# The low part of the next head's FFN weights: two VectorE subtractions in place of four on GpSimd

## The reference

```python
xn = layernorm(x)
q, k, v = (xn @ Wq.T), (xn @ Wk.T), (xn @ Wv.T)          # 16 heads of 32
attn = softmax(causal(q @ k.T / sqrt(32)))
s = (attn @ v) @ Wo.T
hidden = fwht(silu(xn @ W1.T) * (xn @ W3.T))             # [b, t, 2048]
g = silu(hidden @ W2.T)
out = x + s * g
```

## Time and profile before

| what | value |
|---|---|
| median of three runs | 1041.69 us |
| profiled execution, its own time / its span | 1041.96 us / 1040.2 us |
| busy, share of the span: PE / DVE / ACT / POOL | 95% / 69% / 54% / 32% |
| weight loads of PE (PEld) | 76% |
| the two stretches of heads | about 96 to 400 us and 620 to 911 us |
| granted TensorE clock, mean | 0.981 |

### The profile page before, as it was taken

The page is one execution under the profiler, slowest core; times in us unless marked ns, Lnnn a source line. Parts: engine busy times, 40 slices in busy tenths (PEclk is TensorE's granted clock), DMA queues, the critical chain, the costliest instruction groups (busy, mean ns, idle before and its releaser), DMA issues.

```text
span 1040.2 us, 18565 instructions
## 1 busy us (share of the span) xinstructions
PE 989.3 (95%) x6344; PEld 789.4 (76%) x6344; DVE 713.5 (69%) x1438; ACT 562.0 (54%) x1179; POOL 336.7 (32%) x587
## 2 busy tenths in 40 slices
PE   4997899999999998999979999999999999989997
PEld 3875777777777776788858877777878778768886
DVE  7684788888998876734473558888888888633433
ACT  3331577676777766732243326777677777733221
POOL 1996245555544431000000104434343443300000
PEclk9999899999999999999989989999999999989999
DMA  7996422323234203961137921232313222080111
GB/s 243 335 262 211 105 53 72 83 72 83 53 91 105 72 23 97 346 215 50 52 101 272 304 52 52 73 82 73 82 53 89 66 73 52 22 331 33 61 41 40
DMA packets 62349, 118.96 MB, mean 114 GB/s; under 512 B 6064, under 2 KB 23088, under 8 KB 62000
## 3 DMA queue, kind: packets, MB, share of 16 engines
q1 hardware_dynamic: 62256, 117.79, 36.9%
HBM read 75.56 MB, written 41.94 MB: 113 GB/s over the span
## 4 chain that ended last, share of the span: by engine, by line
PE 83%; POOL 7%; DMA 3%; DVE 3%; issue 2%; ACT 1%; SPq 1%; POOLq 0%; DVEq 0%; ACTq 0%
PE f L1198 32%; PE s L1163 8%; PE f L1066 7%; PE f L1068 7%; PE f L1067 7%; PE m L1147 4%; PE o L1179 3%; POOL wht_mid L514 3%; PE o L1181 3%; POOL wht_in L514 3%; PE xs L1147 2%; DMA qk_st<-m_lo 2%; PE m L1066 1%; PE m L1067 1%; PE m L1068 1%
## 5 line engine op out<-in xcount | busy, mean ns | idle before, releaser
L936 DVE TENSOR_TENSOR p_lo<-stage,p_hi 128x512 f16<-128x512 f32 (+2 forms) x288 | 190.5, 664 | 73.3 <-ACT p_hi L662 72.6
L652 ACT ACTIVATE stage<-s 128x512 f32<-128x512 f32 (+2 forms) x288 | 152.0, 528 | 149.5 <-PE s L1163 148.6
L1198 PE MATMUL f<-xt_hi,w_hi 128*128 128x512 f32 x512 | 204.4, 399 | 2.6 <-POOL w_lo L535 2.6
L1198 PE MATMUL f<-xt_lo,w_hi 128*128 128x512 f32 x512 | 204.2, 399 | 0.0
L1198 PE MATMUL f<-xt_hi,w_lo 128*128 128x512 f32 x512 | 204.1, 399 | 0.0
L1163 PE MATMUL s<-qk_st 98*128 98x512 f32 (+2 forms) x384 | 153.6, 400 | 10.8 <-DMA qk_st<-m_lo 8.2
L662 ACT ACTIVATE p_hi<-stage 128x512 f16<-128x512 f32 (+2 forms) x288 | 159.7, 554 | 0.0
L528 POOL TENSOR_SCALAR_AFFINE_SELECT stage<-stage 128x128 f32<-128x128 f32 x192 | 62.9, 328 | 266.3 <-ACT stage L652 266.2
L924 DVE CUSTOM_DVE_ANT_0 m<-m,causal 128x1024 f32<-128x1024 f32 (+3 forms) x128 | 131.3, 1026 | 16.2 <-PE m L1147 15.0
L535 POOL TENSOR_TENSOR w_lo<-w,w_hi 128x256 fp32r<-128x256 f32 x128 | 95.4, 762 | 67.3 <-ACT w_hi L680 47.1
L1198 PEld LDWEIGHTS f<-xt_hi,w_hi 128*128 128x128 f32 x512 | 98.0, 191 | 19.0 <-issue 2.9
(11 more groups left out here) (148 smaller groups left out, 1857.4 us busy)
## 6 DMA issues: line engine op xcount, KB each, us to landing
qk_st<-qk_stacks SPq DMA_DIRECT2D x96, 256.0 KB, 4.4
qk_stacks<-qk_hi SPq DMA_DIRECT2D x64, 256.0 KB, 3.2
w<-w1w SPq DMA_DIRECT2D x32, 512.0 KB, 3.5
qk_stacks<-qk_lo SPq DMA_DIRECT2D x32, 256.0 KB, 3.4
xb<-x SPq DMA_DIRECT2D x8, 512.0 KB, 6.6
wht_in<-w SPq DMA_DIRECT2D x4, 1024.0 KB, 7.8
w_butterflied<-wht_in SPq DMA_DIRECT2D x4, 1024.0 KB, 6.3
stage<-w_butterflied SPq DMA_DIRECT2D x16, 256.0 KB, 3.8
```

The costliest lines, as they stand in the source:

```text
L652: act.activation(expd[q % NE][:, 0:end - need], SB[q % 2][:, 0, need - start:end - start], ACT.Exp).then_inc(exp_done, 1)
L936: dve.tensor_tensor(p_lo[q % NP][:, 0:end - need], expd[q % NE][:, 0:end - need], p_hi[q % NP][:, 0:end - need], ALU.subtract).then_inc(p_ ...
L1198: mm = pe.matmul(F[m][:, 0, :], w, v, start=k == 0, stop=k == GMM - 1)
```

## The change

The four subtractions of 256 columns on GpSimd in each head but the last of a sequence are gone, with the waits for `exp_done` ahead of them. VectorE has two subtractions of 512 columns instead, one in slot 6 and one in slot 7, each behind `probs_lo` and ahead of the denominators, the gate and `hide` of that slot. The first head of each sequence keeps GpSimd, in two pieces of 512 columns instead of four of 256. The counts of `w13_lo_done` go from four to two a head.

```diff
+W13_LOW_AT = [6, 7]
...
             def load_w13(n):
-                after(sp, w13_lo_done, 4 * n)
+                after(sp, w13_lo_done, 2 * n)
                 sp.dma_start(w13[:], w1w3[n % NH]).then_inc(w13_in, 16)
...
             def w13_low(n, piece):
                 pool.wait_ge(w13_hi_done, n + 1)
-                at = (slice(None), piece // 2, slice(piece % 2 * (D // 2), (piece % 2 + 1) * (D // 2)))
-                pool.tensor_tensor(w13_lo[n % 2][at], w13[at], w13_hi[n % 2][at].bitcast(F32), ALU.subtract
-                                   ).then_inc(w13_lo_done, 1)
+                pool.tensor_tensor(w13_lo[n % 2][:, piece, :], w13[:, piece, :],
+                                   w13_hi[n % 2][:, piece, :].bitcast(F32), ALU.subtract).then_inc(w13_lo_done, 1)
...
                     if j > 0:
                         combine(n - 1, 1)
-                    if j + 1 < NH:
-                        for piece in range(4):
-                            pool.wait_ge(exp_done, n * NS + 4 + piece)
-                            w13_low(n + 1, piece)
                     mask(n * NS + 2 * TPC)
...
-                for piece in range(4):
+                for piece in range(2):
                     w13_low(b * NH, piece)
...
+            def w13_low(n, piece):
+                dve.wait_ge(w13_hi_done, n + 1)
+                dve.tensor_tensor(w13_lo[n % 2][:, piece, :], w13[:, piece, :],
+                                  w13_hi[n % 2][:, piece, :].bitcast(F32), ALU.subtract).then_inc(w13_lo_done, 1)
...
                     if 1 <= g <= SLOTS:
                         probs_lo(n0 * NS + g - 1)
+                    if s in W13_LOW_AT and j + 1 < NH:
+                        w13_low(n0 + j + 1, W13_LOW_AT.index(s))
                     if s == COPY_AT[0] and j < NH:
                         denominators(n0 + j, 0)
...
                     if i == 0:
-                        pe.wait_ge(w13_lo_done, 4 * (n + 1))
+                        pe.wait_ge(w13_lo_done, 2 * (n + 1))
```

More of the change, by code:

```diff
@@ L416, in heads @@
                         store_slab(D // P - 1)
-                sp.wait_ge(w13_lo_done, 4 * (n0 + NH))
+                sp.wait_ge(w13_lo_done, 2 * (n0 + NH))
                 sp.dma_start(w13[:], wo[NO * P:KT * P, :].rearrange("(k p) d -> p k d", p=P)
```

## The result

The changed kernel takes 1053.88 us (median of four runs, 1051.70 to 1055.24) where four runs of the kernel before, taken with them, give 1040.95 us (1039.00 to 1044.04). The ratio is 1.0118, with a 95% interval of 1.0095 to 1.0141: slower by 12.9 us. The mean granted TensorE clock is 0.981 in both profiles. The profiled execution took 1055.20 us, with a span of 1053.5 us.

The account below looks back on a forecast made before the run. The prediction took TensorE to bound the heads, with VectorE second. Its terms, 4.2 + 3.2 + 2.8 = 10.2 us on the profiled execution's 1041.96 us, gave 1052 us, with an 8-in-10 range of 1041 to 1068 us.

Parts of the forecast that it names:

- VectorE's part: New operations in slots 6 and 7 delay `m_lo`, for which TensorE waits: 4.2 + 3.2 us.
- the load's part: `load_w13`, released later, is in flight beside the `m_lo` transfer: 0.1 us in each of 28 heads, 2.8 us.
- Case B: Head with 0.44 us of slack: `m_lo` 0.45 to 0.85 us late, TensorE loses 0.2 us, 16 heads, 3.2 us.
- Case A: Head where TensorE already waits for `m_lo`: 0.2 to 0.6 us later, taken as 0.35, 12 heads, 4.2 us.
- there is cover: Other users of late VectorE results don't wait: `p_lo` is used some 3 us later, `hidden` frees its bank early.
- The relief: Without GpSimd's pieces `p_lo` of slot 4 gets 0.3 us shorter, which can shorten the transpose's 3.4 us of waits.
- the slack: First scores come 3.01 us after the `m_lo` transfer's issue, 0.4 us more than the quick transfer's 2.60 us.
- Both stretches of heads longer by about 5 us each: Sign in the changed profile: both sequences' heads grow about equally; the forecast is wrong if only the first grows.
- The start: First head's GpSimd pieces, two of 512 columns instead of four: no difference, 0.2 us either way.
- VectorE becomes the bound: Rival: in the first sequence VectorE reaches 57 to 58 of 60 us busy; 1060 us, chance 0.06.
- The weight load takes the place of the wait: Rival: 512 KB beside the maxima's transfer cost 0.5 us or more a head; 1063 to 1071 us, chance 0.16.
- Faster by the freed port: Rival: relief in slots 4 to 7 and VectorE's idle time cover the 1.22 us a head; 1035 us, chance 0.05.

Follow-up runs that it names:

- e7: Changed kernel with the 1 MB store of the first head issued behind the maxima of the next head; 1049.73 us, ratio 1.0068 to the kernel before.
- e3: Changed kernel with the maxima of the next head stored ahead of the load of the weights; 1046.13 us, ratio 1.0031 to the kernel before.
- e1: Kernel before, GpSimd's pieces kept, with two extra VectorE subtractions into an unread tile in slots 6 and 7; 1054.46 us against 1042.69, ratio 1.0099.
- e10: Changed kernel with the two VectorE operations in slots 3 and 4 and nothing else; 1039.79 us, ratio 0.9968 to the kernel before.
- e2: Kernel before, with only the load of the FFN weights held back until `p_lo` of slot 6 is done; 1047.98 us against 1042.69, ratio 1.0050.
- e4: Changed kernel with the two VectorE operations in slots 4 and 5 instead of 6 and 7; 1045.05 us, ratio 1.0020 to the kernel before.
- e8: Changed kernel with the two VectorE operations in slots 3 and 4 and the 1 MB store behind the maxima; 1038.86 us, ratio 0.9969 to the kernel before.
- e6: The changed kernel, unchanged, run for a second profile; 1053.71 us.

## Why the prediction was right

The time, the sign and the two causes came out as forecast: +12.9 us where 10.2 were summed, within the range. The terms came out less well than their sum: VectorE's part is 4 us below its 7.4, the load's part 6 us above its 2.8. That the two misses nearly cancel is luck. The ratios over the kernel before split the 12.3 us (1.18% of 1041) as follows: from the changed kernel to e7, the store behind the load, 0.50% or 5.2 us; from e7 to e3, the load beside the maxima in the other heads, 0.37% or 3.9 us; what is left in e3, 0.31% or 3.2 us, is VectorE's lateness less its relief. By the intervals the three have uncertainties of about 3, 2.5 and 1.4 us, and the middle and the last also hold whatever it is worth to have the store go out at 101 us. The stretches of the profiles, which leave the first pair out of the last two, give nearly the same split: 4.0 us for the first pair, 3.2 us from the changed kernel to e3, and 3.8 us from the kernel before to e3 in the other heads.

- **VectorE brings `m_lo` late: right, but VectorE's lateness cost 3 us instead of 7.4, and much of it at another place.** Case B, the step from the earlier trace rows, forecast 0.45 to 0.85 us of lateness; that head shows 0.70, and the other heads that had 2.74 us from transpose to `m_lo` show 0.38 to 0.70. Case A, the step from the earlier trace rows, was costed at 0.35 us a head with an argument for 0.05 beside it; the head of the earlier trace rows shows 0.04, and the twelve heads of this kind 0.27 in the mean. The lateness was sized fairly; what it costs was not. On PEld the waits for `m_lo` grew by 2.6 us where 7.4 were summed: by 1.9 us in the twelve heads (4.2 summed), 1.8 of them in four heads alone, and by 0.75 us in three of the others (3.2 summed). Another 2.9 us came up where the prediction had said "there is cover" and that "`hidden` frees its bank a whole FFN group ahead of need": at the FFN products, which wait for the gate and `hide` behind the new operations. In the head of the earlier trace rows the 0.2 us taken for case B are 0.44 us, and they are lost there, not at `m_lo`. That step failed. At the transpose 2.3 us of waits went away in eight heads and 1.0 us came up in two; the sum had put this at nothing. Together the three kinds of wait grew by 4.2 us, not far from the 3.2 and 3.8 us above. In the head of the earlier trace rows the idle 0.48 us and the relief of `p_lo` do carry over to slot 7, as the argument for 0.05 had it. The part that failed in both cases is that the new operation has to wait for GpSimd: the new operation starts first (719.88, `ctx_sum` at 720.09; 830.61, the mask at 830.69), so it is GpSimd that waits (`ctx_sum` 0.89 us where 0.46 stood, the mask 0.76 where 0.29 stood), and the new operation took 0.78 and 0.68.
- **The relief: right in kind, larger than taken.** `p_lo` of slot 4 is at 0.69 us as forecast. The wait at the transpose fell from 3.4 us in ten places on PEld to 2.1 in two, and what is left of it are the first transposes in the heads of each sequence, with 1.03 us each. e1 against e3 prices it: without the relief 0.99%, with it 0.31%. The same shows in the stretches without the first pair, 243.5 and 282.2 us against 241.1 and 277.0, 7.6 us. That the difference of 7 us is the relief is argued, not shown, as the two kernels differ in the order of the queue as well; neither has a load in flight beside the transfer of `m_lo` in these heads.
- **The load beside the maxima's transfer: right in kind, 9 us instead of 2.8.** It was priced at 0.1 us in each of 28 heads. It cost 5.2 us in one head and 3.9 us in few others. The first step that failed is "the queue itself is free again after 0.35 us, so `store_maxima` isn't held". In the head where the 1 MB store goes out behind the load it is held, for 2.74 us, and the transfer then takes 4.44 us. The diff did not touch `store_slab`, but it stands behind `load_w13` in the same order of SyncE, and whatever is behind a wait moves with it. The second step that failed is the slack: the 2.60 us of the earlier trace rows were taken as the quick transfer, which left 0.4 us. By their landings most transfers of `m_lo` in the kernel before take 1.75 to 1.78 us, so an ordinary head has 1.2 us of slack and loses nothing. The loss lies in the heads whose transfer is slow, and there the late `m_lo` and the slower transfer add up. Two of them in the changed kernel, pieces of the chain of work that ended last:

```profile
240.76 3.65 DMA qk_st<-m_lo
...
260.35 4.17 DMA qk_st<-m_lo
```

  They bring the maxima of heads 7 and 8 of sequence one, counted from 0. In the kernel before the same two took 3.30 us (at 234.61) and 2.63 us. In head 7 `m_lo` is 0.45 us later and the transfer 0.35 us longer, and the wait grows by 0.8 us, from 0.65 to 1.43. In head 8 it is 0.40 and 1.54 us, and the wait grows from 0 to 1.76. The second transfer began 2.14 us behind the issue of the load at 258.21. The same heads of sequence two wait 0.6 us at most.

  The landings of `m_lo` in all twelve profiles tell the two things that slow it apart, over the 30 heads behind the first two of sequence one. The first is the load. Where it had landed before `m_lo` was issued, or was issued behind it, and nothing else was in flight (143 transfers), the transfer took 1.75 to 1.78 us; where it landed up to 1.45 us behind the issue, at most 1.85 us; from 1.45 to 1.6 us behind, 1.81 to 1.97 us; up to 1.9 us behind, 2.0 to 2.3 us; up to 2.1 us behind, 2.34 to 2.42 us. The second is a transfer of 8 or 16 KB that the profile lists as `instruction`. All 42 transfers of `m_lo` above 2.42 us (of 360) have one in flight between issue and landing; so do 78 of the other 318, 55 of which are no longer for it. Heads 7 and 8 have one in every kernel, with the load early or late. The row of the DMA queues for the one of head 7 in the kernel before, in the window from 234 to 238 us:

```profile
q8 instruction: 1, 0.02, 1.7%
```

  One such transfer stands also in the windows behind 240.76 and 260.35 of the kernel after. That these transfers are the cause of the slow ones is read from the traces; no run moves them.
- **"Both stretches of heads longer by about 5 us each": wrong.** Sequence one grew by 4.0 + 4.8 us, sequence two by 2.2. With the relief counted the late `m_lo` costs little in any head, and the stalls above 0.7 us at the transfer are all in sequence one. The forecast's marker for the load as the cause, transfers above 3.3 us at line 1163, was met too, but it can't tell: the kernel before has two of them itself, 4.28 and 3.59 us.
- **The signs named.** The waits for `m_lo` are 5.9 us in 15 heads on PEld (3.3 in 12 before; the 1.1 us on PE are three of the same stalls), below the 7 to 12 us in nearly all heads that were forecast; VectorE is busy 22.1 us more (25 to 35 forecast) and GpSimd 68.1 us less (90 forecast), as its mask and `ctx_sum` take longer now; the load is issued 1.57 to 2.38 us ahead of the `m_lo` transfer in the ordinary heads, 2.06 in the mean, where 2 us at most were forecast.
- **The start:** nothing, as forecast (93.6 and 92.3 us against 92.4 and 93.4).
- **The rivals.** "VectorE becomes the bound" falls by e10. "The weight load takes the place of the wait" had the larger cause right and its price too high: it is a few heads, not 28 times 0.5 us. "Faster by the freed port" failed for slots 6 and 7, but in slots 3 and 4 it is what happens: the cover there is the idle time ahead of `p_lo` of slot 4, and 3 us are won.

Open: the stretch between the two sequences, which the change doesn't touch, is 2.4 us longer. It scatters from 234.7 to 237.9 us over the kernels run here, and no run was made for it. Which heads meet an instruction transfer, and whether the place of the code could be chosen so that none falls beside `m_lo`, wasn't tried either.

The Trainium skill (SBUF — State Buffer, Who interferes with whom) says that a VectorE instruction with two inputs in SBUF and a GpSimd instruction that reads SBUF hold each other up, the later one until the earlier one ends. This case's trace agrees, in kind and in size. Over the 128x512 subtractions with two SBUF inputs of the kernels before, after, e1 and e10, those with no GpSimd operation beside them take 0.67 to 0.70 us. One that starts behind a running GpSimd operation with 0.17 us or more left is longer by what is left less 0.13 to 0.15 us in 241 of 263 cases (`p_lo` of slot 4 at 704.58 has 0.44 us left of the pieces and takes 0.99). The other 22 lose nothing: the GpSimd operation had itself started behind a VectorE operation, and VectorE's next one followed at once. A mask or `ctx_sum` that starts behind a running subtraction of this form is longer by what is left of the VectorE operation less some 0.06 us (0.49 us left, 0.43 longer, for `ctx_sum` in 22 heads of the kernel after). The prediction's estimate by the strict rule, 3 us on top of its sum, did not come out for another reason: it took GpSimd to be first in slot 7. The new operation was first, took 699 ns in the mean, 11 ns above the 688 of the earlier trace rows, and the holding up fell on GpSimd, which TensorE doesn't wait for here.

## What to carry to other kernels

Work that moves to another engine moves every wait on its counter, and every transfer that stands behind such a wait in the queue, named in the diff or not: list what the released queue issues next, to the third transfer, and how far in front of a transfer that somebody waits for it now lands. Issue the small urgent transfer ahead of the large one, or release the large one early. Of the engine that receives the work, follow every operation behind the new one to whoever waits for it, the buffers that it frees too. Put the work where the receiving engine has idle time of its own, not where the diff finds room: the same two subtractions cost 12.9 us in slots 6 and 7, about 2 in slots 4 and 5, and win 3 in slots 3 and 4.

## What the runs showed of the hardware

**A large transfer holds up the issue of the next one.** The issue of a 4 KB transfer on SyncE's queue took 0.64 to 0.65 us as a rule, and 2.74 and 2.54 us (after, e2) where 1 MB had been issued 1.3 and 1.5 us before it and 512 KB another 0.4 us before that. With only the 512 KB ahead, by 1.7 us, it took 0.65 us (e7), and with 1 MB ahead by 3.7 us or more too (before, e4, e10). At the very start of the heads, 0.5 us behind the issue of a load of 1 MB, it takes 2.75 to 4.12 us in every kernel. In e8, where the load is 7.9 us ahead of the 1 MB store, the first stack load behind the store is still held until 3.0 us after the store's issue. So the issuing queue itself can be held up, and not only the transfer. No run has the store alone ahead of `m_hi`.

**A small transfer beside others.** The transfer of `m_lo`, 4 KB, takes 1.75 to 1.78 us with nothing else in flight. A load of 512 KB, which takes some 3.5 us, lengthens it only where it lands more than about 1.5 us behind the issue of `m_lo`, by up to 0.6 us. The transfers above 2.42 us all have an instruction transfer beside them (3.30 and 2.63 us in heads 7 and 8 of the kernel before, 3.65 and 4.17 us with the load as well), which the traces show together and no run takes apart.

**GpSimd and VectorE.** The one that starts second is the one that gets longer. `ctx_sum` went from 0.46 to 0.89 us and the mask from 0.29 to 0.76 us behind a running subtraction with two inputs in SBUF; the subtraction itself took 0.86 us behind a running `ctx_sum` in the kernel after and 0.95 us in e10, where 0.69 is usual.

**The clock behind a stall.** In the kernel after, the stall of 3.89 us at 131 us is followed by 12 us at a mean granted clock of 0.86 (0.91 in e6); in the kernel before, with a stall of 1.65 us there, it stays at 1.00 in the same window. At the lower of the two levels, 1.2 GHz of 2.4, that is 1.7 us of work lost on top of the stall.
